# Two attention layers over 128 graphs on one core: from graph pairs with both layers interleaved to quads of graphs, layer after layer, with 512-column projections

## What is computed

```python
def layer0(x, adj, Wq, bq, Wk, bk, Wv, bv, Wo, bo):      # 8 heads of 64
    q, k, v = (heads(x @ W + b) for W, b in ((Wq, bq), (Wk, bk), (Wv, bv)))
    s = einsum('bqhd,bkhd->bhqk', q, k) / 8 + (1.0 - adj) * -1e9
    return einsum('bhqk,bkhd->bqhd', softmax(s), v).reshape(b, n, d) @ Wo + bo

def layer1(x, adj, Wq, bq, Wk, bk, Wv, bv):               # the same without the output projection
    ...
x = layernorm(x + layer0(x, ...))
x = layernorm(x + layer1(x, ...))
```

## Time and profile before

| | us |
|---|---|
| median of 3 runs | 3196.25 (3194.61 to 3197.16) |
| the profiled execution: its own time | 3195.59 |
| the profiled execution: its span | 3193.8 |
| busy in the span: PE / PEld | 3121.4 / 2796.6 |
| busy in the span: DVE / ACT / POOL | 2007.7 / 1683.2 / 1157.1 |
| mean granted TensorE clock | 0.992 of full |
| transfers, mean | 97 GB/s |

### The profile page before, as it was taken

How to read it: one execution, slowest core, us unless ns; L and a number is a source line. 1 busy time by engine, 2 the same in 40 slices (tenths; PEclk the granted TensorE clock), 3 DMA queues, 4 the chain that set the end, 5 groups by cost and what they waited for, 6 DMA issues and landing times.

```text
span 3193.8 us, 78685 instructions
## 1 busy us (share of the span) xinstructions
PE 3121.4 (98%) x25100; PEld 2796.6 (88%) x25100; DVE 2007.7 (63%) x7062; ACT 1683.2 (53%) x5773; POOL 1157.1 (36%) x1093
## 2 busy tenths in 40 slices
PE   6999999999999999999999999999999999999994
PEld 6998898898888888988988888889889889888894
DVE  4566666666666666666666665666666666666654
ACT  4555555555555555555555555555555555555552
POOL 1333333333333333333333333333333333333332
PEclk9999999999999999999999999999999999999997
DMA  4333333333333333333333333333333333333332
GB/s 154 77 103 102 89 100 97 98 92 96 104 94 90 102 101 90 101 101 93 93 97 103 95 90 105 98 91 102 101 90 97 98 101 92 94 104 95 91 99 70
DMA packets 346121, 310.45 MB, mean 97 GB/s; under 512 B 38896, under 2 KB 301296, under 8 KB 346096
## 3 DMA queue, kind: packets, MB, share of 16 engines
q1 hardware_dynamic: 344800, 309.48, 36.6%
q10 hardware_dynamic: 1296, 0.67, 0.1%
HBM read 75.11 MB, written 33.55 MB: 34 GB/s over the span
## 4 chain that ended last, share of the span: by engine, by line
PE 80%; DVE 12%; issue 5%; DVEq 1%; DMA 0%; POOL 0%; ACT 0%; SPq 0%; POOLq 0%
PE ps_proj L371 41%; PE ps_proj L380 29%; PE ps_att L415 6%; PE ps_score L403 4%; DVE prob L778 4%; DVE x_res L869 2%; DVE x L809 2%; DVE stats L793 1%; DVE neg_max L778 1%; DVE xt_hi L741 1%; DVE mean_var L796 0%; DVE inv_sum L786 0%; DVEq L1004 0%; DMA prob<-w_q 0%; DVEq L775 0%
## 5 line engine op out<-in xcount | busy, mean ns | idle before, releaser
L1030 POOL TENSOR_TENSOR prob<-prob,inv_sum 128x512 f32<-128x512 f32 x512 | 525.5, 1042 | 1153.4 <-DVE inv_sum L786 1153.4
L597 ACT ACTIVATE prob<-prob,neg_max 128x128 f32<-128x128 f32 x2048 | 792.8, 391 | 261.3 <-DVE neg_max L778 261.2
L371 PE MATMUL ps_proj<-xt_hi,w_hi_q 128*128 128x256 f32 x2048 | 593.7, 290 | 32.3 <-ACT xt_hi L607 14.3
L371 PE MATMUL ps_proj<-xt_hi,w_lo_q 128*128 128x256 f32 x2048 | 580.6, 283 | 0.0
L371 PE MATMUL ps_proj<-xt_lo,w_hi_q 128*128 128x256 f32 x2048 | 580.4, 283 | 0.0
L371 PE MATMUL ps_proj<-xt_hi,w_hi_k 128*128 128x256 f32 x2048 | 579.7, 283 | 0.0
L371 PE MATMUL ps_proj<-xt_lo,w_hi_k 128*128 128x256 f32 x2048 | 579.6, 283 | 0.0
L371 PE MATMUL ps_proj<-xt_hi,w_lo_k 128*128 128x256 f32 x2048 | 579.3, 283 | 0.0
L778 DVE CUSTOM_DVE_ANT_0 prob<-ps_score,mask 128x128 f32<-128x128 f32 x2048 | 459.5, 283 | 16.5 <-PE ps_score L403 4.8
L819 DVE STREAM_TRANSPOSE blocks_t<-prob 128x512 f32<-128x512 f32 x512 | 341.7, 696 | 200.4 <-DMA prob_t<-blocks_t 164.3
L371 PEld LDWEIGHTS ps_proj<-xt_hi,w_hi_q 128*128 128x128 f32 x2048 | 392.7, 192 | 56.8 <-DVE x_res L869 17.8
(11 more groups left out here) (78 smaller groups left out, 4996.6 us busy)
## 6 DMA issues: line engine op xcount, KB each, us to landing
prob_t<-blocks_t SPq DMA_DIRECT2D x1024, 128.0 KB, 2.7
y<-x_feat SPq DMA_DIRECT2D x128, 256.0 KB, 2.6
x_res<-x_tok SPq DMA_DIRECT2D x64, 512.0 KB, 3.6
prob_t<-prob SPq DMA_DIRECT2D x512, 64.0 KB, 2.1
out<-y SPq DMA_DIRECT2D x128, 256.0 KB, 2.0
prob_t<-blocks_t SPq DMA_DIRECT2D x256, 64.0 KB, 2.1
y<-y SPq DMA_DIRECT2D x256, 64.0 KB, 2.1
prob<-w_q SPq DMA_DIRECT2D x2, 512.0 KB, 7.0
```

The costliest lines, as they stand in the source:

```text
L371: last = pe.matmul(ps_out[:, i * T:(i + 1) * T], wp[:, c, cols], xp[:, c, :], start=(c == 0 and n == 0), stop=(c == NC - 1 and n == 2))
L597: last = act.activation(prob[b][:, i, n, :], prob[b][:, i, n, :], ACT.Exp, bias=neg_max[l][b][:, i, n:n + 1], scale=-1.0, accum_out=row_su ...
L1030: pool.tensor_tensor(prob[b][:, i], prob[b][:, i], inv_sum[l][b][:, i, :].unsqueeze(2).to_broadcast([P, HB, NODES]), ALU.mult).then_inc(no ...
```

## The change

The unit is now a quad, QB = 4 graphs and T = 512 tokens. There are G = 32 quads and 2G + 1 = 65 steps, written out one after the other (no hardware loop): steps 0 to 31 project quads for layer 0, steps 32 to 63 for layer 1, and step s does the attention of step s - 1 between its projections. The eight weight tiles in SBUF serve both layers: layer 1's k, q and v are loaded in steps 31 and 32 into `w_new` and split into the same tiles. The output of layer 0 goes to DRAM twice, as blocks by features (`x1_feat`, four transfers a graph) and by tokens with the value bias added (`x1_tok`), and layer 1 reads both back as layer 0 reads `x_feat` and `x_tok`. The high parts of both layers' inputs are made on VectorE, the low parts on GpSimd. PSUM has a ring of four banks for projections and attention results and two times two banks for scores.

```diff
-GB = 2
-T = GB * NODES
+QB = 4
+T = QB * NODES
...
-                for i, m in enumerate(chunks):
-                    cols = slice(m * P, m * P + P)
-                    for c in range(NC):
-                        parts = [(w_hi[w], xt_hi[l]), (w_hi[w], xt_lo[l]), (w_lo[w], xt_hi[l])]
-                        for n, (wp, xp) in enumerate(parts):
-                            last = pe.matmul(ps_out[:, i * T:(i + 1) * T], wp[:, c, cols], xp[:, c, :],
+                cols = slice(m * P, m * P + P)
+                for c in range(NC):
+                    parts = [(w_hi[slot], xt_hi[par]), (w_hi[slot], xt_lo[par]), (w_lo[slot], xt_hi[par])]
+                    for n, (wp, xp) in enumerate(parts):
+                        last = pe.matmul(ring[bank][:], wp[:, c, cols], xp[:, c, :],
...
+            def attend(a, b, bank, layer):
+                pe.wait_ge(prob_t_in[b], 64 * (a + 1))
+                pe.wait_ge(v_set, QB * a + b + 1)
+                for c in range(NC):
+                    for e in range(2):
+                        h = 2 * c + e
+                        v_head, p_head = v[b][:, h * HD:(h + 1) * HD], by_head(prob_t[b], layer)[:, e, c]
+                        if layer == 0:
+                            last = pe.matmul(ring[bank][e * HD:(e + 1) * HD, c * NODES:(c + 1) * NODES],
+                                             v_head, p_head, start=True, stop=True)
+                        else:
+                            last = pe.matmul(ring[bank][:, h * HD:(h + 1) * HD], p_head.rearrange("p n q -> p (n q)"), v_head,
+                                             start=True, stop=True)
...
+        def by_head(t, layer):
+            if layer == 0:
+                return t[:].rearrange("p n (e c q) -> p e c n q", e=2, c=NC)
+            return t[:].rearrange("p n (q e c) -> p e c n q", e=2, c=NC)
...
+            def residual1(a, b, bank):
...
+                for e in range(2):
+                    last = dve.tensor_tensor(
+                        x1_turned[b % 2][:].rearrange("p (c e d) -> p c e d", c=NC, e=2)[:, :, e, :],
+                        ring[bank][:].rearrange("p (c e d) -> p c e d", c=NC, e=2)[:, :, e, :],
+                        inv_sum[b][:, e, :].unsqueeze(2).to_broadcast([P, NC, HD]), ALU.mult)
+                last.then_inc(scaled_set, 1)
...
+                dve.tensor_tensor(x_res[b][:], x1_turned[b % 2][:], x_res[b][:], ALU.add).then_inc(sum_set, 1)
...
+            def store_x1(a, b):
+                sp.wait_ge(x1_turned_set, QB * a + b + 1)
+                to = x1_feat[a, b].rearrange("(f n) r k -> f n r k", n=BLK)
+                for r in range(BLK):
+                    sp.dma_start(to[:, :, r, :],
+                                 x1_turned[b % 2][r * SQ:(r + 1) * SQ, :].rearrange("p (n k) -> p n k", n=BLK)
+                                 ).then_inc(x1_feat_out[b % 2], 16)
...
+            for s in range(2 * G + 1):
+                step(s, s % 2, None if s > LAST else s // G, None if s == 0 else (s - 1) // G)
```

More of the change, by code:

```diff
@@ L394, in scores, with token_unit @@
-            def scores(l, group, b, banks_free, count):
-                pe.wait_ge(q_set[l], group * 2 + 2)
-                pe.wait_ge(k_set[l], group * 2 + 2)
-                need(pe, banks_free, count + 2 * b + 2)
+            def token_unit(bank, hi, lo, slot, done):
+                for c in range(NC):
+                    parts = [(hi(c), w_hi[slot]), (hi(c), w_lo[slot]), (lo(c), w_hi[slot])]
+                    for n, (xp, wp) in enumerate(parts):
+                        last = pe.matmul(bank[:], xp, wp[:, c, :],
+                                         start=(c == 0 and n == 0), stop=(c == NC - 1 and n == 2))
+                last.then_inc(done, 1)
@@ L399, in scores @@
+            def scores(s, b):
+                pe.wait_ge(q_set, NC * s + NC)
+                pe.wait_ge(k_set, NC * s + NC)
+                need(pe, masked_set, 2 * (QB * s + b) - 2)
                 tok = slice(b * NODES, (b + 1) * NODES)
                 for c in range(NC):
-                    for e in range(HALVES):
+                    for e in range(2):
                         rows = slice(e * HD, (e + 1) * HD)
-                        last = pe.matmul(ps_score[b][e][:, c, :], q_all[rows, c, tok], k_all[rows, c, tok],
+                        last = pe.matmul(ps_score[b % 2][e][:, c, :], q_all[rows, c, tok], k_all[rows, c, tok],
@@ new lines, in exps, with attention_high @@
+            def exps(a, b):
+                for i in range(2):
+                    act.wait_ge(masked_set, 2 * (QB * a + b) + i + 1)
+                    for n in range(NC):
+                        last = act.activation(prob[b][:, i, n, :], prob[b][:, i, n, :], ACT.Exp,
+                                              bias=neg_max[b][:, i, n:n + 1], scale=-1.0,
+                                              accum_out=row_sum[b][:, i, n:n + 1])
+                    last.then_inc(exp_set, 1)
+            def attention_high(a, b, bank):
+                act.wait_ge(att_done, QB * a + b + 1)
+                need(act, wo_done, QB * a + b - 1)
+                act.activation(at_hi[b % 2][:].rearrange("p c n -> p (c n)"), ring[bank][:], ACT.Copy
+                               ).then_inc(at_hi_set, 1)
@@ L1012, in _ @@
+            for b in range(QB):
+                x_high(0, b, 0, first_raw[b])
+            for i in range(4):
+                first_low(i)
+            constants()
+            first_low(4)
+            first_low(5)
+            all_steps(dve, step)
         @block.gpsimd
         def _(pool):
-            def x0_low(group, half):
-                pool.wait_ge(x0_hi_set, group * 2 + half + 1)
-                pool.tensor_tensor(x0_half(xt_lo[0], half), x0_half(xt_raw, half), x0_half(xt_hi[0], half).bitcast(F32),
-                                   ALU.subtract).then_inc(x0_lo_set, 1)
@@ L1103 @@
+            all_steps(pool, step)
 def kernel(**inputs):
```

1395 lines of the change are left out of this document (574 added, 821 removed).

## The result

The changed kernel takes **3455.09 us** in the median of four runs (3453.81 to 3457.45), beside 3195.69 us for the kernel before on the same chip. The ratio is 1.0812 (95% interval 1.0795 to 1.083): 8.1% slower. The prediction was 3146 us with a range of 3033 to 3240. It was wrong, and the time lies beyond its range.

A forecast was written before the change was run, and what follows sets the result against it. PE, busy 98% of the span, was taken as the bound. 32 quads of 97.0 us (3104) plus 41 us of edges gave a 3145 us span; with 1.8 outside it and the median's offset, 3146 us, range 3033 to 3240.

The forecast's parts named there:

- the price of the token attention: Layer 1's attention on PE: 0.115 us an instruction, set by loading 128 columns; bounds 0.06 to 0.172, higher in B.
- B: Rival: layer 1's stationary columns 8 elements apart make a load 0.24 us, total 3402 us (3263 if only overlap fails); chance 0.17.
- 512-column projections: Feature projections: 12,288 matmuls of 0.120 us become 6,144 of 0.227 us, minus 79.9 us.
- No switch around full-array attention: Around layer 1's attention on PE: no array-form switch counted; if it paid the same, 13 us more.
- Layer 1's attention by tokens: 128 graphs x 16 x 0.115 = 235.5 us against 120 for the present form: plus 115 us, the largest term.
- Other engines and waits: DVE, ACT and POOL work hides under PE, counted at nothing; DVE at 71% in layer 1, tightest margin about 1.5 us.
- rival C: New waits on VectorE for masks; 1 us in each of 64 steps gives 3210 us; chance 0.16.
- Through DRAM: Layer 0's stores are read 32 steps later; traffic rises from about 97 to some 115 GB/s; cost zero.
- A2: Rival: the array takes a 128-column load within 0.06 us, layer 1's attention costs 123 us, total 3033 us; chance 0.12.
- Edges: Start, bias product, weight change in step 32 and end of the program: 41 us instead of 76.4, minus 35 us.
- The change does what it says: Possible failures, put into C: a 512-column pitch other than 0.227 us (excluded), and fetching some ten times the instructions (small).

The follow-up runs named there:

- with pairs: Changed kernel with layer 1's probabilities laid out by pairs of heads, so stationary columns lie 2 elements apart: 3144.85 us, ratio to the kernel before 0.9839.
- in the form of before: Changed kernel with layer 1's attention in layer 0's form (values stationary, probabilities moving, two column tiles), its output left in the wrong orientation: 3038.38 us.
- Quarters: Changed kernel with layer 1's stationary operand as 32 contiguous columns in layer 0's layout, results to four column tiles: 3040.20 us, ratio to the kernel before 0.9511.
- the kernel with spread attentions: Changed kernel with layer 1's four attentions one at a time between q units instead of two and two, columns still 8 apart: 3453.82 us.

## Why the prediction was wrong

**The step that failed** is the price of the token attention, "I take 0.115 us, set by the load, between 0.112 and 0.120". It is 0.232 us. 0.115 is right for columns up to 2 apart (0.109 and 0.115 measured). The prediction saw the distance, made a rival of it (B) with 0.24 us a load, and cited the rule that speaks for it; then it gave it 0.17, because "a load draws a column each 0.875 ns, half the rate of the moving operand, which leaves room". There is no such room: a new line costs 1.77 ns on this path, and 0.875 ns a column (0.112 / 128) already is the rate at which a load in a row runs. A rate seen at one access pattern was taken for slack in another. The row nearest to the unknown read was `k_all` on ACT with 0.98 ns an element on top; it gave 0.24 almost exactly, and should have weighed more than the argument from rates. That a write of ScalarE with columns 32 apart and a read of TensorE with columns 8 apart cost so nearly the same extra is, as far as these runs show, luck.

**The second term, in none of the cases,** is the clock: 2.4 us a step, 32 x 2.4 = 77 us. The prediction counted full clock mid-run, as in the earlier trace rows, and gave no reason why it should last. B's 3402 had the price of the load alone, and missed 53 us: 77 for the clock, less 16 since its load was a little too dear (2048 x 0.008), and less some for the edges.

The sum in full, against the predicted span of 3145: a quad takes 52.19 + 54.61 = 106.80 us instead of 97.0, 32 x 9.80 = 313.6; the edges are 3455.6 - 32 x 106.80 = 38.0 instead of 41. So 313.6 - 3.0 = 310.6, and 3145 + 310.6 = 3455.6.

Point by point:

- *512-column projections, 0.227 us:* right. 48 key matmuls take 10.89 us. Layer 0's step came out at 52.19 for 52.3.
- *No switch around full-array attention:* right. From the last k matmul to the block 0.235 us, from its last instruction to the q matmul 0.204.
- *Layer 1's attention by tokens costs 235.5 us against 120 before, plus 115:* right for loads in a row or 2 apart, as the kernels with pairs and in the form of before show (106 us between them for 102); with columns 8 apart it is 2 x 7.42 a step, 475 us.
- *Other engines and waits, nothing (rival C):* right. PE is busy 1250.00 of 1250.00 us in layer 1 (1800 to 3050 us), and 1494.40 of 1500 in layer 0. In the kernel with pairs, where DVE had no slack from a slower PE, the step is still 44.65 for 44.5.
- *Through DRAM, nothing:* right by the same numbers.
- *Loads don't bind (A2):* wrong. In the full array 0.109 us is the floor for 128 columns. Quarters come near A2's 3033 (3040.20), but for another reason: four loads beside each other.
- *Edges, 41 us:* 38.0 here, 43.6 with pairs (3142.5 - 32 x 96.84), 45.2 with quarters. The parts, predicted in brackets: first matmul at 14.32 (13.9); step 0 42.9 us, 5.8 more than its projections and scores (6); step 32 60.1 us, 7.9 above its neighbours (6); from the last step's start at 3374.8 to the end 80.8 us, of which 54.6 are the step and 17.5 a step's share for attention (54.6 less 37.1 for its projections and scores), so 8.7 are left (15). The first three steps of layer 1 are 1.4 us longer than the later ones.
- *The change does what it says:* right, and unrolling cost nothing that any stretch of PE shows.

Other places where a layout shows, off the path: the transposes that write `turned` in layer 1's layout, and ACT's write of `k_all` (32 elements apart), 1208 ns beside 689 for `q_all`.

```profile
L606 DVE STREAM_TRANSPOSE turned<-prob 128x512 f32<-128x512 f32 x181 | 193.0, 1160 | 73.3 <-DMA prob_t<-turned 73.3
L464 ACT ACTIVATE k_all<-ring,bk_col 128x512 f32<-128x512 f32 x90 | 108.7, 1208 | 83.2 <-PE ring L281 83.2
```

(both from layer 1's stretch.) With pairs the mean transpose over both layers is 692 ns, in the changed kernel 928.

## What to carry to other kernels

Before an operand's layout is chosen for the engine that writes it, count the 16-byte lines that TensorE must touch to read it: here a float32 operand with one column on a line cost 1.77 ns a column instead of 0.87 as the stationary operand and 1.9 instead of 0.9 as the moving one, and the engine that binds paid it in each of 2048 instructions. When an access pattern is new to a kernel, price it from the nearest row with such a pattern, and not from the slack of a row that has none. A small product (64 moving columns) belongs into column tiles, whose loads run side by side: here 0.060 us for four quarters against 0.109 for one full load.

## What the runs showed of the hardware

- The price of a load by lines: 0.109, 0.115, 0.169, 0.227 and 0.232 us for columns 1, 2, 3, 4 and 8 float32 elements apart. With columns 4 or 8 apart it is the same at either clock: the block goes on at its pitch where the clock falls to 0.50. With columns 3 apart the pitch rises from 0.173 to 0.213 us there.
- The clock can fall on an engine that is listed as busy all the time (1250.00 of 1250.00 us, clock 0.87): here behind full-array instructions with slow loads, not behind as long a block with cheap ones (1.00). The bill comes afterwards, at the wide matmuls.
- About half of the low clock can vanish without any gain (0.935 to 0.965 in the kernel with spread attentions, 3455.09 and 3453.82 us), when it goes where loads bind. The clock over a span is no measure of its cost.
- Four times as many instructions cost nothing extra where they go to four tiles: 128 in 1.93 us, beside 32 in 3.49 for the full array.
